# Experts' second products from fp32 to three passes of fp16 halves, two steps later

## The reference

```
logits = xf @ gate_w.T
topk_w, idx = top_k(logits, 2)
comb = zeros.at[..., idx].add(softmax(topk_w))
h  = silu(einsum('td,ehd->teh', xf, w1))     # first product, 8 experts, 256 hidden columns
eo = einsum('teh,edh->ted', h, w2)           # second product
routed = einsum('te,ted->td', comb, eo)
shared = silu(xf @ sg_gate.T) * (xf @ sg_up.T) @ sg_down.T
```

## Time and profile before

| | |
|---|---|
| timed runs | 2176.82, 2176.49, 2174.26 us; median 2176.49 |
| profiled execution, its own time | 2176.14 us |
| its span from first to last instruction | 2174.3 us |
| PE busy | 1914.1 us (88%) |
| PEld busy | 1564.8 us (72%) |
| DVE busy | 1475.4 us (68%) |
| ACT busy | 979.1 us (45%) |
| POOL busy | 838.9 us (39%) |
| mean granted TensorE clock | 0.951 |

### The profile page before, as it was taken

One profiled execution on the slowest core, in us unless ns is written; L12 is line 12 of the kernel. 1 busy time (PEld: TensorE's weight loads), 2 busy tenths in 40 slices (PEclk: granted clock), 3 DMA queues, 4 the chain that ended last, 5 costly groups with the idle time before them and its releaser, 6 DMA issues.

```text
span 2174.3 us, 50901 instructions
## 1 busy us (share of the span) xinstructions
PE 1914.1 (88%) x18448; PEld 1564.8 (72%) x18448; DVE 1475.4 (68%) x5011; ACT 979.1 (45%) x2557; POOL 838.9 (39%) x726
## 2 busy tenths in 40 slices
PE   3687999999999999999999999999997787499981
PEld 2576787888788878887887888787875565377771
DVE  5685465768677867777777677776767767676661
ACT  2353545545455545454546464636454462022210
POOL 1000001113434333433334242526253456668885
PEclk9899999999999999999999999999998998699886
DMA  6773754444344434433343334232400001167775
GB/s 217 244 283 116 255 185 157 133 153 142 94 141 125 137 84 133 120 117 99 122 126 109 90 97 134 84 102 83 132 13 5 10 5 25 29 111 113 115 112 74
DMA packets 165766, 251.52 MB, mean 116 GB/s; under 512 B 65502, under 2 KB 121216, under 8 KB 164777
## 3 DMA queue, kind: packets, MB, share of 16 engines
q10 hardware_dynamic: 43656, 153.58, 22.0%
q0 software_dynamic: 54752, 50.97, 11.0%
q1 hardware_dynamic: 67136, 44.03, 7.7%
HBM read 203.15 MB, written 85.27 MB: 133 GB/s over the span
## 4 chain that ended last, share of the span: by engine, by line
PE 69%; DVE 9%; issue 8%; ACT 5%; POOL 4%; DMA 3%; ACTq 1%; SPq 0%; DVEq 0%; POOLq 0%
PE W L1065 35%; PE Cb L1065 21%; PE L L1065 5%; PE W L1238 5%; POOL slots_dram L980 3%; PE L L1093 1%; ACT area_b L1496 1%; DVE ring L2216 1%; DMA ring<-filters_dram 1%; DMA odd_sum_dram<-qv 1%; ACT xh L1580 1%; ACTq L1690 1%; DMA band<-band_dram 1%; PE W L1225 1%; ACT seq_hi L1507 1%
## 5 line engine op out<-in xcount | busy, mean ns | idle before, releaser
L1065 PE MATMUL Cb<-seq_hi,ring 128*128 128x174 f16 x4356 | 571.5, 239 | 18.2 <-DVE seq_lo L1810 10.4
L1065 PE MATMUL Cb<-seq_lo,ring 128*128 128x174 f16 x2178 | 504.9, 239 | 0.0
L980 POOL DMA_INDIRECT slots_dram<-rows,slot_i x360 | 428.9, 1191 | 101.8 <-issue 101.8
L1065 PEld LDWEIGHTS Cb<-seq_hi,ring 128*128 128x128 f16 x4356 | 385.5, 97 | 50.6 <-DVE seq_lo L1810 11.1
L973 POOL TENSOR_TENSOR h<-h,xh 115x384 f32<-115x384 f32 x120 | 120.5, 1004 | 646.3 <-ACT xh L1580 645.7
L1624 ACT ACTIVATE area_k<-W 115x345 f32<-115x345 f32 x384 | 176.4, 459 | 294.2 <-PE W L1238 292.7
L2084 DVE CUSTOM_DVE_ANT_0 area_h<-W,offsets 115x345 f32<-115x345 f32 x384 | 196.2, 514 | 109.7 <-PE W L1065 99.4
L1065 PE MATMUL W<-area_k,qv 64*115 64x345 f16 (+1 forms) x1920 | 253.0, 380 | 4.2 <-ACT area_k L1624 2.6
L2068 DVE SCALAR_TENSOR_TENSOR area_h<-area_h,W 128x345 f32<-128x345 f32 x256 | 131.1, 513 | 182.6 <-ACT area_h L1570 176.8
L1618 ACT ACTIVATE area_h<-area_h,nmax 115x345 f32<-115x345 f32 x384 | 224.9, 586 | 26.1 <-DVE nmax L2084 25.3
L1065 PEld LDWEIGHTS Cb<-seq_lo,ring 128*128 128x128 f16 x2178 | 211.9, 97 | 14.0 <-issue 0.3
(11 more groups left out here) (287 smaller groups left out, 3365.0 us busy)
## 6 DMA issues: line engine op xcount, KB each, us to landing
ring<-filters_dram ACTq DMA_DIRECT2D x252, 512.0 KB, 3.9
slots_dram<-in_empty_slots POOLq DMA_DIRECT2D x8, 1544.0 KB, 14.8
area_k<-slots_dram SPq DMA_DIRECT2D x64, 193.0 KB
filters_dram<-ring ACTq DMA_DIRECT2D x24, 512.0 KB, 4.8
band<-band_dram SPq DMA_DIRECT2D x64, 189.0 KB, 3.3
filters_dram<-offsets ACTq DMA_DIRECT2D x12, 512.0 KB, 4.4
slots_dram<-rows,slot_i POOLq DMA_INDIRECT x360
x_win<-in_xpad SPq DMA_DIRECT2D x16, 252.0 KB
```

What stands on the lines that cost most here:

```text
L980: pool.indirect_dma_start(out=slots_d, out_offset=bass.IndirectOffsetOnAxis(ap=slot_i[parity(b)][:, m:m + 1], axis=0), in_=rows[parity(b)] ...
L1065: return pe.matmul(o, l, r, start=start, stop=stop)
```

## The change

The hidden columns of the experts and the weights `w2` become pairs of fp16 numbers, a high half (the value rounded) and a low half (the rest rounded). The product is high x high, high x low and low x high, accumulated in fp32: 18 fp16 matmuls in place of 6 fp32 ones. The weights are scaled by 16, which `comb` takes back. The shared expert stays fp32.

VectorE's `hidden` now writes its result back into `th`. One step later ScalarE copies it to fp16 (`hidden_high`), and GpSimd subtracts that copy from `th` into the low half (`hidden_low`). `tanh_in` waits for the low half two blocks before, since it writes into the same `th`. The experts' `down` stands three steps behind the second hidden block and no longer one (in the last iteration three and no longer two). GpSimd's queue goes by steps: a low half and one scatter in each of 16 steps, an add and one scatter for each expert; in the last iteration 16 times a low half and a scatter. The weights of `step_load` follow the new price of a product.

The fp32 weights are no longer loaded with the layer's other weights (one transfer of 1 MB from ScalarE's queue in the setup). In iteration 0, behind its other work, SP loads them in two halves into a free area; ScalarE rounds them in steps 6 and 14 and VectorE makes the low halves in steps 7 and 15. SP's second load waits for VectorE's first low half.

```diff
@@ class Order
+        self.split = {hid_step(n) + 1: n for n in range(2 * E0)}
-FULL = Order(lambda n: 1 + 4 * n // 3, 1, 2, [...], 6, 9)
+FULL = Order(lambda n: 1 + 4 * n // 3, 3, 2, [...], 6, 9)
-ALONE = Order(lambda n: n, 2, 2, ...)
+ALONE = Order(lambda n: n, 3, 2, ...)
@@ step_load
-    t = lone_step(s) + 1.36 * (s in FULL.down)
+    t = lone_step(s) + (1.05 if FULL.down.get(s, E0) < E0 else 1.36 if s in FULL.down else 0)
@@ build
-        w2eT = sb("w2eT", [128, E0 * 2, C])
+        w2e_hl = sb("w2e_hl", [128, 2, E0 * 2, C], F16)
-        hid = area_h[:, 0:4 * TOK].rearrange("p (j n) -> p j n", j=4)
+        hid_shared = area_h[:, 0:2 * TOK].rearrange("p (j n) -> p j n", j=2)
+        hid_hl = area_h[:, 0:4 * TOK].bitcast(F16).rearrange("p (j x n) -> p j x n", j=4, x=2)
+        w2e_stage = area_h[:, 0:E0 * C]
@@ SP, end of iteration
+                if isinstance(ro.b, int) and ro.b == 0:
+                    for n in range(2):
+                        sp.wait_ge(s_setup, 1)
+                        if n:
+                            sp.wait_ge(s_w2lo, n)
+                        sp.dma_start(w2e_stage, dram["w2eT"][:, n * E0:(n + 1) * E0, :].rearrange("p k c -> p (k c)"))\
+                            .then_inc(s_w2in, 16)
@@ GpSimd
+            def hidden_low(ro, n):
+                pool.wait_ge(hid_hi.h, hid_hi.at(ro.f, n + 1))
+                j = 2 * (n // 2 % 2) + n % 2
+                pool.tensor_tensor(hid_hl[:, j, 1, :], th[:, n % 2, :], hid_hl[:, j, 0, :], ALU.subtract).then_inc(hid_lo.h, 1)
@@ GpSimd, last iteration
-                    scatter(ro.send, SENDS // 3, SENDS - SENDS // 3)
+                    for n in range(2 * E0):
+                        hidden_low(ro, n)
+                        scatter(ro.send, SENDS // 3 + n, 1)
@@ GpSimd, full iteration
-                for e in range(E0):
+                at = 0
+                for s in range(STEPS):
+                    if ro.l is not None and s == 9:
+                        power(ro.l, 2, 1)
+                    if ro.f is not None and s in ro.order.split:
+                        hidden_low(ro, ro.order.split[s])
+                        if ro.send is not None:
+                            scatter(ro.send, at, 1)
+                            at += 1
+                    e = ro.order.mixed.get(s, E0)
+                    if e == E0:
+                        continue
                     if ro.f is not None:
                         add_expert(ro.f, e)
-                    if ro.l is not None and e == 1:
-                        power(ro.l, 2, 1)
-                    if ro.send is not None:
-                        scatter(ro.send, e * SENDS // E0, SENDS // E0)
+                        if ro.send is not None:
+                            scatter(ro.send, at, 1)
+                            at += 1
@@ TensorE, down
-                pe.wait_ge(hid_ready.h, hid_ready.at(ro.f, 2 * e + 2))
+                if e < E0:
+                    pe.wait_ge(hid_lo.h, hid_lo.at(ro.f, 2 * e + 2))
+                    if e == 0:
+                        pe.wait_ge(s_w2lo, 2)
...
+                            for n, (x, w) in enumerate([(0, 0), (0, 1), (1, 0)]):
+                                last = mm(y, hid_hl[:, 2 * (e % 2) + c, x, part], w2e_hl[:, w, 2 * e + c, :],
+                                          start=(c == 0 and n == 0), stop=(c == 1 and n == 2))
@@ ScalarE
-                if n >= 2:
-                    act.wait_ge(hid_ready.h, hid_ready.at(ro.f, n - 1))
+                if 2 <= n < 2 * E0 + 2:
+                    act.wait_ge(hid_lo.h, hid_lo.at(ro.f, n - 1))
+            def hidden_high(ro, n):
+                e = n // 2
+                if e >= 2:
+                    wait_full(act, ro, ("Y", e - 2))
+                act.wait_ge(hid_ready.h, hid_ready.at(ro.f, n + 1))
+                act.activation(hid_hl[:, 2 * (e % 2) + n % 2, 0, :], th[:, n % 2, :], ACT.Copy).then_inc(hid_hi.h, 1)
@@ ScalarE, step s: behind the copy of the transposed scores
+                    if ro.f is not None and s in ro.order.split:
+                        hidden_high(ro, ro.order.split[s])
                     if ro.f is not None and s in ro.order.hid:
                         tanh_in(ro, ro.order.hid[s])
+                    if isinstance(ro.b, int) and ro.b == 0 and s in (6, 14):
+                        n = (6, 14).index(s)
+                        act.wait_ge(s_w2in, 16 * (n + 1))
+                        act.activation(w2e_hl[:, 0, n * E0:(n + 1) * E0, :].rearrange("p k c -> p (k c)"), w2e_stage, ACT.Copy,
+                                       scale=WS).then_inc(s_w2hi, 1)
@@ VectorE
-                    dve.scalar_tensor_tensor(dst, th[:, n % 2, :], 1.0, bank[:, 0:TOK], ALU.add, ALU.mult)\
+                    dve.scalar_tensor_tensor(th[:, n % 2, :], th[:, n % 2, :], 1.0, bank[:, 0:TOK], ALU.add, ALU.mult)\
```

More of the change, by code:

```diff
@@ L103, in __init__ @@
         self.ln2, self.gate = ln2, gate
-FULL = Order(lambda n: 1 + 4 * n // 3, 1, 2, [-12, -10, -7, 1, 2, 3, 4, 5, 6, 7, 8, 9, 10, 11, 12, 13, 14, 16, 18, 20, 22, 23, 24, 25], 6, 9)
+FULL = Order(lambda n: 1 + 4 * n // 3, 3, 2, [-12, -10, -7, 1, 2, 3, 4, 5, 6, 7, 8, 9, 10, 11, 12, 13, 14, 16, 18, 20, 22, 23, 24, 25], 6, 9)
 EARLY = [-2 - len(PROJ), -1 - len(PROJ)]
-ALONE = Order(lambda n: n, 2, 2, EARLY + list(range(-15, -6)) + [0, 2, 4, 6, 7, 8, 9, 10, 11, 12, 13, 15, 16], 2, 4)
+ALONE = Order(lambda n: n, 3, 2, EARLY + list(range(-15, -6)) + [0, 2, 4, 6, 7, 8, 9, 10, 11, 12, 13, 15, 16], 2, 4)
 def unit(u):
@@ L603, in build @@
         hid_ready = Signal("hid_ready", NHID)
+        hid_hi = Signal("hid_hi_ready", 2 * E0)
+        hid_lo = Signal("hid_lo_ready", 2 * E0)
+        s_w2in = ctx.enter_context(nc.semaphore("expert_weights_loaded"))
+        s_w2hi = ctx.enter_context(nc.semaphore("expert_weights_hi_ready"))
+        s_w2lo = ctx.enter_context(nc.semaphore("expert_weights_lo_ready"))
         comb_ready = Signal("comb_ready")
@@ L702, in build @@
                        (q_b, dram["q_b"]), (k_b, dram["k_b"]), (v_b, dram["v_b"]), (peT, dram["peT"]), (wposT, dram["wposT"]), (woT, dram["woT"]), (bo, dram["bo"].partition_broadcast(A)),
-                       (gate0T, dram["gate0T"]), (w2eT, dram["w2eT"]),
+                       (gate0T, dram["gate0T"]),
                        (sdT, dram["sdT"]), (winT, dram["winT"]),
@@ L1298, in down @@
             def down(ro, e):
-                pe.wait_ge(hid_ready.h, hid_ready.at(ro.f, 2 * e + 2))
+                if e < E0:
+                    pe.wait_ge(hid_lo.h, hid_lo.at(ro.f, 2 * e + 2))
+                    if e == 0:
+                        pe.wait_ge(s_w2lo, 2)
+                else:
+                    pe.wait_ge(hid_ready.h, hid_ready.at(ro.f, NHID))
                 def products(bank):
                     for j in range(J):
+                        y, part = bank[0:A, j * C:(j + 1) * C], slice(j * A, (j + 1) * A)
                         for c in range(2):
-                            wt = w2eT[:, 2 * e + c, :] if e < E0 else sdT[:, c, :]
-                            last = mm(bank[0:A, j * C:(j + 1) * C], hid[:, 2 * (e % 2) + c, j * A:(j + 1) * A], wt,
-                                      start=(c == 0), stop=(c == 1))
+                            if e == E0:
+                                last = mm(y, hid_shared[:, c, part], sdT[:, c, :], start=(c == 0), stop=(c == 1))
+                                continue
+                            for n, (x, w) in enumerate([(0, 0), (0, 1), (1, 0)]):
+                                last = mm(y, hid_hl[:, 2 * (e % 2) + c, x, part], w2e_hl[:, w, 2 * e + c, :],
+                                          start=(c == 0 and n == 0), stop=(c == 1 and n == 2))
                     return last
@@ L2055, in gate_weights @@
                 c3 = comb[:, :].rearrange("p (j g) -> p j g", g=8)
[L2056 removed]
+                dve.scalar_tensor_tensor(c3, c3, 0.5 / WS ** 2, spread8(gsum), ALU.mult, ALU.mult).then_inc(comb_ready.h, 1)
                 dve.wait_ge(comb_ready.h, comb_ready.at(ro.f, 1))
@@ L2181, in iteration @@
                         hidden(ro, ro.order.hid[s])
+                    if isinstance(ro.b, int) and ro.b == 0 and s in (7, 15):
+                        n = (7, 15).index(s)
+                        dve.wait_ge(s_w2hi, n + 1)
+                        part = slice(n * E0, (n + 1) * E0)
+                        dve.scalar_tensor_tensor(w2e_hl[:, 1, part, :].rearrange("p k c -> p (k c)"), w2e_stage, WS,
+                                                 w2e_hl[:, 0, part, :].rearrange("p k c -> p (k c)"), ALU.mult, ALU.subtract)\
+                            .then_inc(s_w2lo, 1)
                     if ro.a is not None and s < UNITS and s % 2 == 0:
```

6 lines of the change are left out of this document (2 added, 4 removed).

## The result

The changed kernel takes 2261.4 us (median; 2258.6 to 2262.2), the kernel before beside it 2176.1 us: ratio 1.0387, 95% interval 1.0374 to 1.0400. It is 85 us slower; 2171 us (2157 to 2189) was predicted. The profiled span is 2256.8 us, 82.5 longer than before.

What follows compares the result with a forecast made beforehand. TensorE's own work was taken to bound batches 1 to 13. From 2176.14 us: -28 in the middle, +10.5 batch 0, +11.5 last iteration, +0.5 second rounding gave 2170.6, with 0.35 then 2171 us; range 2157 to 2189.

Steps and rivals of the forecast that it cites:

- The second product: TensorE, middle batches: 18 fp16 matmuls take 1.05 us instead of 1.34, 104 times, a gain of 30 us.
- rival (c): Second product on TensorE: load and stream don't overlap with 115 columns, -30 becomes +16, 2217 us; chance 0.04.
- What the two steps of delay take away: TensorE, middle: the product's 7.2 us of waits for VectorE's hidden columns should go.
- GpSimd's queue, middle: Low half 0.90 us; 50 of 52 us filled in steps 2 to 20, no stall on TensorE, 0 charged.
- rival (b): Steps 2 to 20: GpSimd becomes the bound from 1.05 us a low half; 2187 or 2208 us; chance 0.11.
- VectorE's hidden operation only changes its target, cost nothing: VectorE, each hidden column block: writing the result to another place adds no time.
- ScalarE and VectorE: Middle: ScalarE's 16 fp16 copies a batch start tanh 0.5 us later; 9 us charged, between 0 and 18.
- rival (a): End of each batch: ScalarE's high half lengthens the path exp, high, tanh, hidden, maximum; 2184 us; chance 0.16.
- Batch 0: New stall: ScalarE waits for the first half of the weights, TensorE loses 10.5 us (8.5 to 12.5).
- Rival (d): Batch 0: no stall, because the band write lands early without the ring loads; 2161 us; chance 0.12.
- The last iteration: GpSimd's 16 scatters each get a low half ahead, so the next scatters start 11.5 us later (9 to 18).
- (e): Saved TensorE time turns into waits for the ring or VectorE, both stalls stay; 2190 to 2198 us; chance 0.05.

Runs made afterwards that it cites:

- e13: e10 with one bank planner number changed (bank rule): an odd unit's scores keep their bank 2 units longer, not 1; ratio 1.0094.
- e18: e15 without GpSimd's subtractions: GpSimd signals at once and the product reads the high half in the low half's place; ratio 1.0057.
- e3: Kernel before, product still fp32, with only the experts' second product two steps later (the adds move with it); ratio 1.0292.
- e10: e3 with GpSimd's root for the next batch's first normalization between the last add and its scatters, not behind them; ratio 1.0170.
- e9: Kernel before, products in place, only scaled sums, adds and what follows in GpSimd's queue two steps later; product's bank kept 5 units longer; ratio 1.0430.
- e11: Kernel before, fp32 product, with the second product one step later instead of two; ratio 1.0184.
- e1: Changed kernel without GpSimd's 256 subtractions: GpSimd signals at once, the product reads the high half in the low half's place; ratio 1.0222.
- e15: Changed kernel with the first weight half loaded early, the root between last add and its scatter, and the planner's 2 for 1 (bank rule); ratio 1.0153.
- e8: Changed kernel with the first half of the experts' weights loaded ahead of batch 0's window load and band write on SyncE; ratio 1.0322.
- e19: e15 with the last iteration's 16 low halves on VectorE and GpSimd sending its 16 scatters there without them; ratio 1.0155.

## Why the prediction was wrong, by its steps

**The second product** was right: 1.00 to 1.10 us for 1.05 (the upper bound of its gain was added up wrong: 0.0525 us each gives 38 us, not 34). Load and stream overlap with 115 columns too, so rival (c) is out. That the gain is real shows in e13 against e18, which have the same place of the product, the same root and the same bank rule: fp32 takes 1463.4 us for 14 batches, the 16-bit form with ScalarE's copies (and without subtractions) 1441.8. The two also differ in where GpSimd's scatters stand and in the planner's weight for a product, and by the medians they are 11 us apart in all where the profiled executions are 17.5. So the 21.6 us, or some 15, are of the size of 30 less the 9 that I charged for ScalarE; that they divide so is not shown.

**"What the two steps of delay take away"** is the step that failed. I looked only at who had waited for the product's input (7.2 us) and charged nothing for the move. It costs 63.1 us in e3, where only the product's steps change, and with them what is tied to them (sums, adds, banks, the convolution's layout). Of these 23.3 are a queue that I named for nobody: the root behind the last add, on GpSimd (e10). 15.5 are two transposes on the bank of two late maxima, which the product used to cover (e13). About 24 stay open; other bank neighbours and the later scaled sums in ScalarE's queue are candidates, and e9 and e11 don't separate them. In the changed kernel the same move shows in other shares: the root 6.6 us, the bank pairings 37.6, where the two transposes wait 43.0 us in ten batches and in e3 28.7.

**GpSimd's queue, middle, "0 charged".** The price of a low half was right (0.892 for 0.90 us), and rival (b) as I put it, a full queue, did not come: 56 of 108 us busy. But the work reaches VectorE. In 1095 us of the trace of after, VectorE's short operations on SBUF are 51 us longer than their usual length (over the lower quartile of each kind, by 0.1 us and more): 14 us during subtractions, 26 during adds, 10 during scatters; in before it is 3 us in all. Leaving the subtractions out doesn't undo it. By a count of the same kind that also keeps different shapes apart (58 us in after, 8 in before) 43 us stay in e1, nearly all during adds, and the later product alone (e3) has 22: most of it comes with the adds at the places where they now stand. The groups that show it best:

```profile
L2225 DVE TENSOR_SCALAR prec_hl<-prec 115x6 f16<-115x6 f32 x64 | 32.5, 507 | 2.2
L2120 DVE SCALAR_TENSOR_TENSOR area_h<-area_h,W 128x345 f32<-128x345 f32 x256 | 131.6, 514 | 176.7 <-ACT area_h L1611 172.4 <-DVE h L2149 1.0
```

The first, on SBUF alone, took 179 ns in before (its median in after is 176: a minority of the 64 are held, the longest 1.8 us); the second, which reads PSUM and SBUF, 513 ns in both. "VectorE's hidden operation only changes its target, cost nothing" was true of that operation and left out its neighbours. The Trainium skill, GPSIMD Engine Reference, "Specifications", says that GpSimd's SBUF interfaces are shared with VectorE, with contention for instructions in a mode with two ports or with two SBUF inputs. The rows agree as far as they go: VectorE's operations on two SBUF tiles are held (tlo and gl above, 0.76 to 0.90 us for 0.20), and the operation with one side in PSUM isn't; in which mode the held TENSOR_SCALAR ran no run shows. The rule was there to be weighed. Yet in e15 VectorE is held just as long (55 us) and the 14 batches take 1454.8 us: what is held matters only through what waits for it.

**ScalarE and VectorE, 9 us.** No wait of TensorE for the high half appears, and that for the exponential is 4.7 us in ten batches, 9.5 in eleven before. But the maximum that TensorE waits for stands behind the high half on the very path that rival (a) names, and no run leaves ScalarE's copies out: the size of this term, and rival (a)'s share of the late maximum, stay open.

**Batch 0** was right in place, cause and size: ScalarE waited 13.0 us for the first half of the weights and TensorE 11.5 (10.5 predicted, 8.5 to 12.5), as timelines of ScalarE and TensorE of after show beside the earlier trace rows:

```profile
236.02 1.06 ACT L1683 ACTIVATE w2e_hl<-area_h 128x1024 f16<-128x1024 f32 x1 [13.02 <-DMA area_h<-in_w2eT]
```

```profile
237.69 0.93 PE L1270 MATMUL W<-ident,area_h 115*115 115x115 f32 x3 [11.47 <-ACT area_h L1667]
```

Rival (d) is out. But taking the early stall away gave only 4.2 us (e8), since a wait of 5.0 us took its place.

**The last iteration** was right in size: the first of the 24 scatters comes 66.1 us after the last add, before 55.6, so +10.5 for +11.5. The reason was half of it. As predicted, the low halves are waited for there: TensorE's products wait 8.1 us in 6 places, ScalarE's tanh 4.7 us in 9 (and 3.1 us in the two iterations before). But it isn't GpSimd's queue alone: with that queue as before, 7 of the 10 us stay (e19, with VectorE's 16 operations more). Without the subtraction anywhere, GpSimd waiting for the high half only, the scatter still comes at 60.6 (e18).

**The rivals.** By its mechanism (e) came nearest: it had the saved time turn into waits for VectorE, at 2190 to 2198, and I gave it 0.05. The only losses in the middle were (c)'s from the matmuls and (b)'s from a full queue, 2208 to 2217, neither of which came and both of which the range left out; none had a loss from the product's place. **The sum by experiments**, from after to the kernel of e18: early load 4.2 us, root 6.3, bank rule 40.5, subtractions 25.1, together 76 of the 82.5 us (by the medians 5.6, 7.1, 40.3 and 21.0, together 74 of 85). The kernel that is left then has a product that is 0.3 us shorter 104 times and is still 6 us slower in its span (12 by its ratio). No version here beats before.

## What to carry to other kernels

When a piece of work moves to a later step on the busiest engine, ask what it covered where it stood: look for the wait that is not in the trace, such as a bank or buffer that its producer frees while the moved work runs. Then follow everything that is tied to the moved piece by order alone (here a root behind the last add in GpSimd's queue), and everything that a planner places from its steps. One experiment with only the move, before any of the arithmetic changes, would have told the sign.

## What the runs showed of the hardware

While GpSimd ran a vector operation of 0.8 to 1.0 us or a scatter of 1.2, some short VectorE operations on SBUF (115x24 and 115x48) took 0.76 to 0.90 us where they otherwise take 0.20, and ended 0.05 to 0.25 us after GpSimd's did; where a scatter and an add follow each other, one of 115x6 lasted up to 1.8 us in after. The operation of 128x345 that reads one side from PSUM kept its 0.51 us. An fp16 product of 18 matmuls with 115 stationary and 128 moving columns runs at 0.055 to 0.061 us each.
